# One kernel, many small edits: weights turned on the host, router logits computed with the residual, slot products in exact bf16 pieces, and new instruction orders

## The reference

```python
x = x + tanh(g_xattn) * smoothquant_mlp(layernorm(x), gate_up_w, down_w)   # per batch, its own weights
x = x + tanh(g_ffn)   * moe(layernorm(x), w_gate, w1, w2)                  # 8 experts, top 1
```

## Time and profile before

| | us |
|---|---|
| Median of 3 runs (115.22 to 115.84) | 115.48 |
| The profiled execution | 115.32 |
| Its span, from first to last instruction | 113.6 |
| First matmul of the experts | 53.27 |
| PE busy in the span | 100.7 |
| DVE, ACT, POOL busy | 85.1, 72.8, 55.9 |

### The profile page before, as it was taken

One profiled execution on the slowest core, in us unless ns is written; L12 is line 12 of the kernel. 1 busy time (PEld: TensorE's weight loads), 2 busy tenths in 40 slices (PEclk: granted clock), 3 DMA queues, 4 the chain that ended last, 5 costly groups with the idle time before them and its releaser, 6 DMA issues.

```text
span 113.6 us, 2268 instructions
## 1 busy us (share of the span) xinstructions
PE 100.7 (89%) x748; PEld 85.2 (75%) x748; DVE 85.1 (75%) x254; ACT 72.8 (64%) x159; POOL 55.9 (49%) x116
## 2 busy tenths in 40 slices
PE   0997979697999979998999999999999999999910
PEld 0265649485766857894989999998999999898800
DVE  1599999989996998956647089997976759396330
ACT  5064998899999897514453798483956848494000
POOL 7065698567999678848776000522310405040131
PEclk9999999999999999999999999999999999999999
DMA  4999899898548121401388898999998100001011
GB/s 35 344 345 239 341 359 357 250 405 274 208 80 295 61 97 43 172 0 45 100 277 291 297 342 308 347 409 337 410 388 289 45 0 20 32 3 46 0 46 46
DMA packets 14091, 22.67 MB, mean 200 GB/s; under 512 B 1287, under 2 KB 11527, under 8 KB 13056
## 3 DMA queue, kind: packets, MB, share of 16 engines
q1 hardware_dynamic: 13312, 20.46, 53.1%
q0 software_dynamic: 768, 2.07, 5.6%
HBM read 20.46 MB, written 2.10 MB: 199 GB/s over the span
## 4 chain that ended last, share of the span: by engine, by line
PE 57%; DVE 22%; DMA 8%; ACT 4%; issue 3%; POOL 2%; POOLq 1%; SPq 1%; DVEq 0%
PE bk L1386 22%; PE bk L1397 13%; PE bk L1399 7%; DMA gr<-out,gidx 5%; DVE am L754 4%; DMA cw<-in_ctx_gu 3%; DVE am L717 2%; PE bk L1306 2%; PE bk L1332 2%; DVE am L710 2%; DVE wide_a L775 2%; PE bk L1362 1%; DVE ra L741 1%; PE bk L1372 1%; DVE q1s L762 1%
## 5 line engine op out<-in xcount | busy, mean ns | idle before, releaser
L467 POOL DMA_INDIRECT out<-xrow,sidx x8 | 10.9, 1357 | 38.6 <-DVE xrow L1001 38.6
L1397 PE MATMUL bk<-w2p,hh 128*128 128x512 f32 x64 | 23.4, 405 | 0.2 <-DVE hl L989 0.2
L1386 PE MATMUL bk<-rows_w,w_sb 128*128 128x128 f32 x192 | 23.2, 275 | 0.2 <-DVE rows_w L950 0.2
L1386 PEld LDWEIGHTS bk<-rows_w,w_sb 128*128 128x128 f32 x192 | 22.3, 192 | 0.9 <-DVE rows_w L950 0.6
L1399 PE MATMUL bk<-w2p,hl 128*128 128x256 f32 x64 | 17.9, 280 | 0.0
L982 DVE TENSOR_TENSOR w2p<-w_sb,w2p 128x1024 fp32r<-128x1024 f32 x12 | 14.2, 1220 | 3.5 <-ACT w2p L560 3.3
L560 ACT ACTIVATE w2p<-w_sb 128x1024 fp32r<-128x1024 f32 x12 | 12.2, 1056 | 4.9 <-PE bk L1399 4.9
L574 ACT ACTIVATE bk<-bk 128x512 f32<-128x512 f32 x16 | 9.3, 583 | 8.8 <-PE bk L1386 8.8
L989 DVE TENSOR_TENSOR hl<-bk,hh 128x512 fp32r<-128x512 f32 x16 | 10.7, 686 | 4.9 <-ACT hh L581 4.9
L1397 PEld LDWEIGHTS bk<-w2p,hh 128*128 128x128 f32 x64 | 12.0, 188 | 2.8 <-issue 0.3
L1192 PE MATMUL bk<-identb,upper 128*128 128x512 bf16 x28 | 9.8, 459 | 2.7 <-POOL upper L300 2.7
(11 more groups left out here) (164 smaller groups left out, 230.3 us busy)
## 6 DMA issues: line engine op xcount, KB each, us to landing
w_sb<-in_w SPq DMA_DIRECT2D x12, 1024.0 KB, 6.1
x<-in_x SPq DMA_DIRECT2D x4, 256.0 KB, 3.8
cw<-in_ctx_gu SPq DMA_DIRECT2D x4, 256.0 KB, 5.5
cw<-in_w SPq DMA_DIRECT2D x1, 1024.0 KB, 5.5
out<-x SPq DMA_DIRECT2D x4, 256.0 KB, 2.1
x<-in_w SPq DMA_DIRECT2D x1, 1024.0 KB
wide_a<-in_w SPq DMA_DIRECT2D x1, 1024.0 KB, 6.8
wide_b<-in_w SPq DMA_DIRECT2D x1, 1024.0 KB, 9.0
```

Source lines behind the costliest of these rows:

```text
L467: nc.gpsimd.indirect_dma_start(out_rows, bass.IndirectOffsetOnAxis(ap=sidx[:, e:e + 1], axis=0), yo[:, e % 2, :], None, bounds_check=B * T ...
L1386: ins = nc.tensor.matmul(HB[e % 2][:, m, n * C:(n + 1) * C], wv[:, k, f:f + P], xgT[:, e % B, k], start=(k == 0), stop=(k == K - 1))
L1397: nc.tensor.matmul(YB[e % 2], hh[:, e % 2, n], w2p[:, e % 2, n].rearrange("p a d -> p (a d)"), start=(n == 0), stop=False)
```

## The change

The host now hands over both weight tensors of the quantised layer turned, so `turn_w` and `down_turn` are gone with the semaphores that they raised. `amax_w` and `scale1` read the weight where it was loaded (SBUF), and one `damax` with one `dguard`, `drecip` and `dfloor` serves all four batches, right after `ratio1(3)`. The loaded x has 9 spare columns for each token row, into which POOL (`row_part`) puts the router's part; `add_x` then makes 265 columns at once and `logit_rows` is gone. Loads of x and stores of x1 now move 1 KB pieces instead of 2 KB ones. `norm1(0)` moves from ACT to DVE. `ratio1` becomes a product and a maximum over both halves at once (`product_w`, `ratio1`).

`hotc` becomes bf16. Token numbers are split into two bf16 parts, the second layernorm's scales and the gates into three, so that `index`, `scales` and `slot_gates` are bf16 products; the parts are added again by a small reduction (`slot_scales`, `slot_gates_out`). `scales` is one block of 8 products at the end. The scales of expert 0 ride in 2 more columns of `sort`, which therefore waits for `rsd`.

The orders on DVE, ACT, POOL and PE are new, and there are 44 constant products instead of 28.

In the diff, the second `norm1` is DVE's, `scale_pieces` runs on POOL ahead of the gathers, the four lines on `chosen_p` end `softmax`, and the last two pieces are from the lists of PE and of DVE.

```diff
-                act.wait_ge(shift1_ready, b + 1)
+                act.wait_ge(shift1_ready, b + 0)
...
-                    last = nc.scalar.activation(xs1[:, b, c], bk[b][:, a, k * T:(k + 1) * T],
+                    last = nc.scalar.activation(xs1[:, b, c], (bk[b][:, 0, k * T:(k + 1) * T], cw[:, b, k])[a],
...
-                nc.scalar.activation(aw[:, b, 1], bk[b][:, 1, 0:D], ACT.Identity,
+                nc.scalar.activation(aw[:, b, 1], dw[:, b], ACT.Identity,
...
+            def norm1(b):
+                dve.wait_ge(rstd1_ready, b + 1)
+                for j in range(J):
+                    last = nc.vector.tensor_scalar(xn[:, b, j], x[:, b, j, 0:D], mv1[:, b, j, 0:1], rs1[:, b, j:j + 1],
+                                                   ALU.subtract, ALU.mult)
...
+            def damax():
+                dve.wait_ge(dw_here, 16)
+                done["damax"] = mark(nc.vector.tensor_reduce(amd[:], dw[:], AX, ALU.max, apply_absolute_value=True))
...
-                    ins = nc.vector.scalar_tensor_tensor(out=x1[:, b, j], in0=bk[b][:, j, 0:D], scalar=q2g[:, b, j:j + 1],
-                                                         in1=x[:, b, j], op0=ALU.mult, op1=ALU.add)
+                    ins = nc.vector.scalar_tensor_tensor(out=x1[:, b, j, 0:D + G], in0=bk[b][:, j, 0:D + G],
+                                                         scalar=q2g[:, b, j:j + 1], in1=x[:, b, j], op0=ALU.mult,
+                                                         op1=ALU.add)
...
+            def scale_pieces():
+                pool.wait_ge(shift2_ready, B)
+                link(nc.gpsimd.tensor_copy(rs_p[:, :, :, 0], rsd))
+                link(nc.gpsimd.tensor_tensor(rs_a[:, :, :, 0], rsd, rs_p[:, :, :, 0], ALU.subtract))
+                link(nc.gpsimd.tensor_copy(rs_p[:, :, :, 1], rs_a[:, :, :, 0]))
+                nc.gpsimd.tensor_tensor(rs_p[:, :, :, 2], rs_a[:, :, :, 0], rs_p[:, :, :, 1], ALU.subtract)
...
-                nc.vector.tensor_scalar(xg[:, 0], XD, rsx[:, 0, 0:1], rsx[:, 1, 0:1], ALU.mult,
+                link(nc.vector.tensor_copy(rs0[:], XD[:, D + G:H]))
+                nc.vector.tensor_scalar(xg[:, 0], XD[:, 0:D], rs0[:, 0:1], rs0[:, 1:2], ALU.mult,
...
+                link(nc.vector.tensor_copy(chosen_p[:, :, 0], chosen[:]))
+                link(nc.vector.tensor_tensor(chosen[:], chosen[:], chosen_p[:, :, 0], ALU.subtract))
+                link(nc.vector.tensor_copy(chosen_p[:, :, 1], chosen[:]))
+                nc.vector.tensor_tensor(chosen_p[:, :, 2], chosen[:], chosen_p[:, :, 1], ALU.subtract)
...
-                link(nc.vector.tensor_scalar(gt[:], GT, tg[:, 1:2], None, ALU.mult))
+                link(nc.vector.tensor_reduce(gsum[:], GT.rearrange("p (c e) -> p e c", c=3), AX, ALU.add))
+                link(nc.vector.tensor_scalar(gt[:], gsum[:], tg[:, 1:2], None, ALU.mult))
...
             hidden(1, 0)
-            slots_turn(2)
             hidden(1, 1)
+            slots_turn(2)
             expert_out(0, 1)
...
-            expert_in(3)
...
             slot_gates_out()
-            hidden_low(1, 0)
             hidden_low(1, 1)
+            expert_in(3)
```

More of the change, by code:

```diff
@@ L24, in gated_smoothquant_moe_kernel @@
     G = E + 1
-    assert (T, D, I, C) == (256, 256, P, P) and ctx_in.shape[1] == 2 * I
+    assert (T, D, I, C) == (256, 256, P, P) and ctx_in.shape[2] == 2 * I
     EPS, LN_EPS, QMAX = 1e-6, 1e-5, 127.0
@@ L1050, in _ @@
+            recip_w(3)
+            guard2(1, 1)
+            product_w(3)
+            floor_w(3)
+            recip2(1, 1)
+            ratio1(3)
+            damax()
             amax2(2, 1)
-            floor_w(3)
-            amax_x(3)
+            gate_up(0, 0)
+            gate_up(0, 1)
+            amax2(2, 0)
             guard2(2, 1)
-            ratio1(3)
+            guard2(2, 0)
             recip2(2, 1)
-            amax2(2, 0)
-            damax(0)
-            guard2(2, 0)
-            dguard(0)
+            dguard()
@@ L1103, in _ @@
             recip4(2)
-            amax3(3)
-            ratio2(3)
-            logit_rows(0)
+            add_x(0)
             lmax_(0)
@@ L1109, in _ @@
             pmax_(0)
-            add_x(0)
             amax4(3)
@@ L1114, in _ @@
             recip4(3)
-            logit_rows(1)
+            split_low(0, 0)
             token(0)
+            loc_(0)
+            hot0_(0)
+            hotc_(0)
+            add_x(1)
             lmax_(1)
-            hot0_(0)
-            loc_(0)
-            add_x(1)
-            logit_rows(2)
-            hotc_(0)
-            lmax_(2)
-            prio_(2)
             prio_(1)
-            pmax_(2)
             pmax_(1)
             onehot_(1)
-            ovr(0)
             add_x(2)
+            loc_(1)
+            lmax_(2)
+            hotc_(1)
+            prio_(2)
+            hot0_(1)
+            pmax_(2)
+            add_x(3)
             onehot_(2)
+            lmax_(3)
             token(1)
-            loc_(1)
-            hot0_(1)
-            logit_rows(3)
-            hot0_(2)
-            lmax_(3)
-            add_x(3)
             prio_(3)
-            ovr(1)
+            token(2)
             pmax_(3)
@@ L1143, in _ @@
             onehot_(3)
-            hotc_(1)
             hotc_(2)
+            token(3)
+            hot0_(2)
             loc_(3)
-            token(2)
+            hot0_(3)
             hotc_(3)
-            ovr(2)
-            hot0_(3)
-            token(3)
-            ovr(3)
             gather_index()
             relative_logits()
-            slot_scales()
+            ovr()
             first_in()
```

495 lines of the change are left out of this document (234 added, 261 removed).

## The result

The changed kernel takes 117.84 us (median of 4, 117.74 to 118.03), the kernel before beside it 115.66: ratio 1.020, 95% interval 1.017 to 1.024. It is slower, by more than forecast (116.6), and just outside the range (114.7 to 117.7). The profiled execution took 117.84 with a span of 116.0, 2.4 more than before.

What follows compares the result with a forecast made beforehand. ACT was taken to bound the quantised layer, a latency chain routing, and TensorE everything from the first hidden product on; 0.2 - 0.8 + 0.9 + 0.95 = +1.25 on 115.32 gave 116.6 us, range 114.7 to 117.7.

Steps and rivals of the forecast that it cites:

- a new wait at slots_turn(3): Expert half: TensorE waits 2.45 us behind slot_gates for expert_in(3) on DVE; +0.95 us (0 to 1.6).
- S: Start of the first hidden product, at 53.27 us in the profile before, forecast at 53.6.
- nothing gives it back, for behind it come products only: Behind slots_turn(3): TensorE's wait of 2.45 us there is not made up, since only products follow.
- fourth stretch: From S to the end: shorter slot_gates and other gains against the wait at slots_turn(3); +0.95 us (0 to 1.6).
- The index: From product2(3) to gidx: logits in one pass, index in bf16 right behind hotc_(3); -0.8 us (-1.3 to 0).
- From the index to S: From gidx to the first hidden product: a second sort step, scales(3) gone, a copy added; +0.9 us (0.6 to 1.2).
- To product2(3): Quantised layer, up to product2(3): ACT sets the pace; +0.2 us (-1.4 to +1.2).
- ACT's start: Start of ACT's long run, 11.44 before: 0.3 us later (0 to 0.8) through norm1(0) on DVE.
- the faster tier: norm1(0) on DVE at two elements a cycle, under 0.3 us each: 0.25 us less at ACT's start, 116.35; no own chance.
- first rival: Quantised layer: DVE, not ACT, sets the pace; product2(3) at -1.4 instead of +0.2, 115.0 us in all; chance 0.23.
- ACT has the less room: Quantised layer, 25 to 30 us: ACT busy 4.96 of 5 us, DVE 4.82, so ACT was taken as limiting.
- the constant products ahead of turn_x(0): Rival at the start: the first 14 hold turn_x(0) by a us, carried to S, 117.6 us; chance 0.13.

Runs made afterwards that it cites:

- e1_in_early: Changed kernel with expert_in(3) on DVE moved up right behind expert_in(2), ahead of slot_gates_out and hidden_low(1,1): 115.18 us, ratio 0.996.
- e3_before_in_late: Kernel before, with only expert_in(3) moved behind slot_gates_out and both hidden_low of expert 1: 121.08 us, ratio 1.036.
- e4_turn2_first: Changed kernel with slots_turn(2) put back ahead of hidden(1,1) on TensorE, expert_in(3) left late: 117.07 us, ratio 1.013.
- e2_products_in_wait: Changed kernel with nine more constant products between slot_gates and slots_turn(3), DVE's order untouched: 117.09 us, ratio 1.012.
- e10_norm0_act: Changed kernel with expert_in(2), expert_in(3) and slots_turn(2) earlier, GpSimd's old multiply-and-add form for image 3, and norm1(0) back on ACT: 112.84 us, ratio 0.973.
- e5_norm3_form: e1_in_early with GpSimd's normalisation of image 3 back in the old multiply-and-add form: 113.30 us, ratio 0.981.
- e7_norm0_first: e1_in_early with norm1(0) ahead of bn(2) on DVE and 12 instead of 14 constant products ahead of turn_x(0): 113.96 us, ratio 0.988.

## Why the prediction was wrong

**Right: sign and mechanism.** I put a new wait at slots_turn(3), because expert_in(3) stands behind slot_gates_out and ACT's turned(2) is late. It is there, with the releaser named, 2.19 us for 2.45. Taking it away alone (e1_in_early: S to slots_turn(3) 1.73 shorter, with 0.35 more idle time of another kind) and making it alone in the kernel before (e3_before_in_late: 2.1 longer) gave its size. That ACT's turned(2) adds to it fits the trace (S + 10.18 for the S + 9.5 to 9.9 put), but no run shows it: in e4_turn2_first the copy did not move. slot_gates took 0.35, as put. slots_turn(3) came at S + 15.71 for S + 15.4, since slot_gates ended at S + 13.53 for 12.95.

**The step that failed: "nothing gives it back, for behind it come products only".** That is true of waiting, and it overlooked what the pause does to the products themselves. Behind a stop of 2.19 us TensorE's clock fell to 1.2 GHz for 3.4 us, which is +1.69 that no term of my sum has. e2_products_in_wait shows it by itself: same wait, no pause, no fall, 40.74 us to the end instead of 42.35; e3_before_in_late made pause and fall in the kernel before. My fourth stretch counts pauses only as time. The profile before had no pause of this size in its expert half, so no row there could show the price. The Trainium skill (TensorE: Matmul & The Clock Gate, "HAM oscillation — how this bites in real kernels") says that idle gaps between bursts of products bring the lower clock back and that the next burst pays for it; in kind the trace agrees, at a shorter wait than that page's example has. It should have been a term with a bound of its own.

**Too dark by 0.8: S.** Forecast +0.3, measured -0.51. The index came 1.22 earlier behind product2(3), not 0.8. From the index to S it was +0.60, not +0.9. To product2(3) +0.11 for +0.2. ACT's start was +0.36 for +0.3 put, but the match says little: the start of the changed orders came at 11.74 to 12.54 from trace to trace, and with norm1(0) back on ACT (e10_norm0_act) it was still at 11.83. norm1(0)'s instructions took 0.40 each, so that the faster tier of the Trainium skill (VectorE: DVE Perf Modes, "The perf-mode tier table") does not show in this trace.

**Hidden inside that +0.1: luck.** Two errors of mine cancelled. The batch-3 normalisation on GpSimd, which I passed over as the same two instructions, was 1.07 us dearer on the path (e5_norm3_form). From ACT's first scale1 to product2(3) the kernel before takes 32.36 us, the changed one 32.11, and with the old form it is 31.04. So 1.3 us were to be had in this stretch, near the 1.6 of my first rival (DVE sets the pace), and one operation on GpSimd hid 1.07 of them. The sum came out right by luck. My "ACT has the less room" went by busy time. The page's fourth part, the chain of work that ended last (each step followed back to what released it), speaks for DVE; by engine, before and then after:

```profile
PE 57%; DVE 22%; DMA 8%; ACT 4%; issue 3%; POOL 2%; POOLq 1%; SPq 1%; DVEq 0%
PE 54%; DVE 22%; POOL 8%; issue 4%; DMA 4%; ACT 3%; SPq 1%; POOLq 1%; DVEq 0%; ACTq 0%
```

From ACT's first scale1 to product2(3) the chain of the kernel before holds 19.5 us of DVE and 4.3 of ACT; that of the changed kernel 13.2 of DVE, 9.3 of POOL and 0.9 of ACT. No run took damax alone back, so how much of the 1.3 is its gain stays open.

**The sum.** 0.2 - 0.8 + 0.9 + 0.95 = +1.25 was forecast; 0.11 - 1.22 + 0.60 + 1.24 + 1.69 = +2.42 is what the traces show. Without the clock's term the time would have been about 116.15, half a us under the forecast. Among the rivals, the constant products ahead of turn_x(0) held it by nothing (it waited 0.20 for DVE), and no gain of 1.6 arrived.

## What to carry to other kernels

Where an edit opens a wait on TensorE in a half that TensorE bounds, price it twice: the wait, and the clock behind it. Here 2.2 us of standing still cost 1.7 more, and nine constant products in it (or one DVE step moved out of the way) saved that. The price is a risk and not a rule: as long a pause elsewhere cost nothing. When a producer is moved behind work that waits for another engine, ask who is waiting for it: a 0.40 us step, placed behind slot_gates_out and hidden_low(1, 1), cost more than all that the rest of the change saved. Which engine sets the pace of a stretch is read from the chain of releasers, not from busy shares. And an operation that "stays the same" with other operands is an operation to price anew.

## What the runs showed of the hardware

- TensorE's clock and its pauses, each from one profiled execution. The clock fell to 1.2 GHz behind waits of 2.19 us (changed kernel) and 1.97 us (e3_before_in_late) in the expert half, worth 1.7 and 1.6 us; behind 2.31 us (e7_norm0_first) and 1.41 us (e2_products_in_wait) ahead of turn_x(3); and in e7_norm0_first at about 9.7, behind 1.27 us ahead of turn_x(0) and inside a second wait of 0.63. It stayed up behind 2.21 us (e5_norm3_form) and 1.68 us (e1_in_early) ahead of turn_x(0), behind 1.59 us in e4_turn2_first, and behind 1.40 us ahead of turn_x(3) in four traces. In e3_before_in_late it also fell at 49.2 us with no idle time above 0.60 in the 9 us before. So the length of a pause alone does not tell whether the clock falls, and no run here shows what else enters.
- GpSimd, tensor_scalar on 128x256 fp32: 1230 ns as subtract and multiply, 557 ns as multiply and add, the scalars one for each partition in both, with the same DVE work beside them.
- GpSimd, tensor_scalar on 128x2: 1.27 us beside a DVE tensor_tensor with two SBUF sources, 0.29 alone.
- Constant products in waits: nine of them in the wait at slots_turn(3) kept the clock up and delayed nothing there (2.54 us from slot_gates' start to slots_turn(3) with them, 2.53 without). Without 27 of the 44, four executions had mean clocks of 0.86 to 0.97, with them six had 0.985 to 0.998; few, and the kernel before went down to 0.93 on that chip too.
